# A transformer block on one core: the last channel half of the result in pieces of 384 and 128 columns in place of 256 and 256, the stores of both shared out over two queues

## The chip, the cores and the metric

The kernel runs on one core of one Trainium2 chip. The metric is the device time of one execution in microseconds (us). The kernel before took 307.04 us as the median of three timed runs (306.98, 307.04 and 307.05).

## What is computed

A small causal convolution with a per-channel filter is added to x, and a conditioned transformer block (modulated layer norm, attention with 16 heads, modulated layer norm, feed-forward net with GELU) is added to that. Cut to what the change touches, the end of it:

```python
x = x + gate1 * attn_out
x2 = _ln(x) * (1.0 + scale2) + shift2
h = jax.nn.gelu(x2 @ ffn_w1 + ffn_b1, approximate=False)
x = x + gate2 * (h @ ffn_w2 + ffn_b2)
return x
# and around it, with x of 32 batches x 32 tokens x 256 channels:
x = x + _L0_cond_ref(x, cond_2048[:, None, :])
x = x + _L1_cond_ref(x, cond_2048, ...)
```

## The kernel before

Everything is kept with channels on the partitions: the 256 channels are two channel halves of 128 (index `ct`), the 1024 tokens are two token halves of 512 (index `n`). The engines' streams are written out by hand and tied together by semaphores, so the order of the code is the order of each engine.

A product with more than 11 bits of mantissa is built from three TensorE products of rounded values (type `F32R`): low weights times high activations, high weights times low activations, high times high. In the second product of the feed-forward net (`ffn2`, lines 1241 to 1243) these three run for each of the eight hidden tiles k, so that one piece of the result costs 24 matmuls, each with a weight load of its own of 128 x 128 elements, all adding into one bank.

The result is made in five pieces, listed in `FFN2_PIECES` (line 206): token half 0 in two pieces of 512 columns (one for each channel half), token half 1 with channel half 0 in one of 512, and token half 1 with channel half 1 in two pieces of 256 columns, the first into bank `YB[1]`, the second into `PB[0]`. TensorE runs pieces 2, 3 and 4 one after another at the very end, with no wait between them. The two last are called the front piece (3) and the back piece (4) here.

When a piece's last matmul is done, VectorE works on it with three instructions: `gated` adds the bias and multiplies by the gate (line 889), then adds the residual (line 895), and `turn` transposes blocks of 32 x 32 into `turned` (line 900) and raises `s_turn`. VectorE takes the pieces in order, 2, 3, 4, and has nothing else at the end.

`store_blocks` (line 213) writes one of the four 32-channel strips of a piece to HBM; a piece thus needs four DMAs, each of 32 partitions, cut into runs of 128 bytes. The stores of pieces 0 to 2 are issued by SP (SyncE) as soon as `s_turn` allows. Of the front piece all four are issued by ACT (ScalarE), which has no other work left; of the back piece two are issued by SP and two by ACT, behind ACT's four of the front piece. The last instruction of SP waits until all 20 stores have landed.

Of the kernel before, what the change touches and what calls it, by code (L numbers as in the profile page):

```python
# [11 lines left out]
P = 128  # L12
# [4 lines left out]
def cond_resid_block_kernel(nc, x, cond, ada_w, ada_b, qkv_w, qkv_b, out_w, out_b,  # L17
# [5 lines left out]
    B, T, C = x.shape  # L23
# [7 lines left out]
    HT = TOK // HALVES  # L31
# [39 lines left out]
    with ExitStack() as ctx:  # L71
# [3 lines left out]
        def sem(name):  # L75
            return ctx.enter_context(nc.semaphore(name))
# [57 lines left out]
        PB, S_BANK, OB, YB = banks[0:3], banks[3], banks[4:6], banks[6:8]  # L134
# [33 lines left out]
        s_turn = sem("result_blocks_turned")  # L168
# [22 lines left out]
        def ln_sq(n, ct):  # L191
            if n < NC:
# [9 lines left out]
        ADA_BANKS = [PB[0][:, P:2 * P], S_BANK[:, 2 * P:3 * P], S_BANK[:, 3 * P:4 * P]]  # L202
        ADA_STEPS = [1, 3, 4]

        ALL, FRONT, BACK = slice(0, HT), slice(0, HT // 2), slice(HT // 2, HT)
        FFN2_PIECES = [(0, 0, YB[0][:, ALL], ALL), (0, 1, YB[1][:, ALL], ALL), (1, 0, YB[0][:, ALL], ALL),
                       (1, 1, YB[1][:, FRONT], FRONT), (1, 1, PB[0][:, FRONT], BACK)]

        x_v = x.rearrange("(n q) t c -> (q t) n c", q=QB)
        out_v = out.rearrange("(n q) t c -> (q t) n c", q=QB)  # L210
# [2 lines left out]
        def store_blocks(eng, n, ct, i, toks):  # L213

            b0, b1 = (n * HT + toks.start) // T, (n * HT + toks.stop) // T
            c0 = ct * P + T * i
            eng.dma_start(out[b0:b1, :, c0:c0 + T].rearrange("b t c -> t b c"),
                          turned[T * i:T * (i + 1), CT * n + ct, toks].rearrange("t (b c) -> t b c", c=T))\
                .then_inc(s_out, 16)
# [3 lines left out]
        @block.sync  # L223
        def _(sp):
            def load_x(n):
                t0, nt = CHUNKS[n][0] // P, CHUNKS[n][1] // P
                sp.dma_start(xtok[:, t0:t0 + nt, :], x_v[:, t0:t0 + nt, :]).then_inc(s_x[n], 16)

            def load_adaw(i, c0, c1):
                sp.dma_start(adaw[:, :, c0:c1], ada_w.rearrange("(k p) n -> p k n", p=P)[:, :, c0:c1])\  # L230
                    .then_inc(s_adaw[i], 16)

            def load_qkv(U, i):
                if U:
                    sp.wait_ge(s_wlo[i], 2 * U)
                c0 = (U % NG) * PIECE + i * INNER
                sp.dma_start(raw[:, 1024 * i:1024 * (i + 1)].rearrange("p (k n) -> p k n", k=CT),
                             qkv_v[:, :, c0:c0 + PIECE]).then_inc(s_raw[i], 16)

            def load_out(U):  # L240
                if U:
                    sp.wait_ge(s_wlo[3], 2 * U)
                r0 = (U % NG) * PIECE
                sp.dma_start(raw[:, 3072:4096].rearrange("p (h n) -> p h n", h=GH),
                             out_w[r0:r0 + PIECE, :].rearrange("(h p) n -> p h n", p=P)).then_inc(s_raw[3], 16)

            load_x(0)
            load_x(1)
            load_adaw(0, 0, ADA1 * P)
            load_x(2)  # L250
            for at, src in ((B_QKV, qkv_b), (B_ADA, ada_b), (B_OUT, out_b), (B_F1, ffn_b1), (B_F2, ffn_b2)):
                n = src.shape[0] // P
                sp.dma_start(rows[at:at + n, :], src.rearrange("(n p) -> n p", p=P)).then_inc(s_row[1], 16)
            for i in range(3):
                load_qkv(0, i)
            load_out(0)
            load_adaw(1, ADA1 * P, ADA * P)
            for U in range(1, NU):
                for i in range(3):
                    load_qkv(U, i)  # L260
                load_out(U)

            w1_v = ffn_w1.rearrange("(k p) n -> p k n", p=P)
            w2_v = ffn_w2.rearrange("(k p) n -> p k n", p=P)
            for i in range(3):
                if i == 2:
                    sp.wait_ge(s_xs, CT)
                    for c in range(CT):
                        sp.dma_start(late_raw[:, c, :].rearrange("p (k n) -> p k n", k=2),
                                     w2_v[:, 4 + 2 * c:6 + 2 * c, :]).then_inc(s_late, 16)  # L270
                sp.wait_ge(s_wlo[i], 2 * NU)
                dst = raw[:, 1024 * i:1024 * (i + 1)]
                if i < 2:
                    sp.dma_start(dst, w1_v[:, i, :]).then_inc(s_raw[i], 16)
                else:
                    sp.dma_start(dst.rearrange("p (k n) -> p k n", k=4), w2_v[:, 0:4, :]).then_inc(s_raw[i], 16)

            for n, ct in ((0, 0), (0, 1), (1, 0)):
                sp.wait_ge(s_turn, CT * n + ct + 1)
                for i in range(P // T):  # L280
                    store_blocks(sp, n, ct, i, ALL)
            sp.wait_ge(s_turn, 5)
            for i in range(2):
                store_blocks(sp, 1, 1, i, BACK)
            sp.wait_ge(s_out, 16 * (5 * P // T))

        @block.gpsimd
# [79 lines left out]
        def _(a):  # L367
# [148 lines left out]
            def hidden(n, m):  # L516
                a.wait_ge(s_f1, MT * n + m + 1)

                if MT * n + m >= 4:
                    a.wait_ge(s_hlo[m % 2], (MT * n + m - 4) // 2 + 1)  # L520
                a.activation(hf[:, m % 4, :], PB[m % 3][:, :], ACT.Gelu,
                             bias=bT[:, B_F1 + m:B_F1 + m + 1]).then_inc(s_hf, 1)
                a.wait_ge(s_hf, MT * n + m + 1)
                a.activation(hh[:, m, :], hf[:, m % 4, :], ACT.Copy).then_inc(s_hhi, 1)
# [16 lines left out]
            x1_high(4)  # L541
            for m in range(MT):
                hidden(1, m)
            a.wait_ge(s_turn, 4)
            for i in range(P // T):
                store_blocks(a, 1, 1, i, FRONT)
            a.wait_ge(s_turn, 5)
            for i in range(2, P // T):
                store_blocks(a, 1, 1, i, BACK)

        @block.vector
        def _(v):
# [750 lines left out]
```

## Time and profile before

| | us |
|---|---|
| median of the timed runs | 307.04 |
| the profiled execution | 307.26 |
| its span, first to last instruction | 305.4 |
| TensorE busy | 298.0 (98%) |
| weight loads busy | 251.5 (82%) |
| VectorE busy | 181.3 (59%) |
| ScalarE busy | 172.5 (56%) |
| GpSimd busy | 121.4 (40%) |

The profile gives busy times of each engine, the chain of work that ended last, and with the trace behind it every instruction's start and duration. The granted clock of TensorE was 1.00 (2.4 GHz) over the stretch in question. The profiled execution took 307.26 us, 1.8 us more than its span of 305.4 us; it is 0.22 us above the median of the timed runs.

### The profile page before, as it was taken

The numbers are of one execution on the slowest core, as the hardware profiler recorded it, in microseconds if no ns is written. First come the engines' busy times: TensorE is split into PE (matmuls) and PEld (weight loads), VectorE is DVE, ScalarE is ACT, GpSimd is POOL, SyncE is SP. The second block draws the span as 40 slices with busy tenths as digits, with TensorE's granted clock in tenths as the row PEclk, the third lists the DMA queues.
The fourth block names the chain that finished last, engine by engine and source line by source line (L and its number), as shares of the span: only waits on it lengthen the run. The fifth ranks groups of instructions, "written<-read, shape, count | busy, mean of one in ns | idle before, by whom it ended". The sixth has DMA issues, their size and how long they took to land.

```text
span 305.4 us, 6186 instructions
## 1 busy us (share of the span) xinstructions
PE 298.0 (98%) x2608; PEld 251.5 (82%) x2608; DVE 181.3 (59%) x315; ACT 172.5 (56%) x313; POOL 121.4 (40%) x104
## 2 busy tenths in 40 slices
PE   7999999999999999999999999999999999999994
PEld 7886987878898888888888888888888888878884
DVE  3996697997866648462446673350721364758433
ACT  5943477534762766475377736743763694624910
POOL 5205839331911552173327134630816381310410
PEclk9999999999999999999999999999999999999999
DMA  7902332500160062007003400430090000000304
GB/s 230 368 31 70 105 104 65 145 0 2 38 239 0 4 196 80 2 2 275 3 2 101 176 0 2 162 115 0 4 338 6 2 0 3 0 1 2 69 0 69
DMA packets 22427, 23.00 MB, mean 75 GB/s; under 512 B 9240, under 2 KB 15488, under 8 KB 22400
## 3 DMA queue, kind: packets, MB, share of 16 engines
q1 hardware_dynamic: 20720, 22.39, 22.6%
q10 hardware_dynamic: 1680, 0.23, 0.4%
q8 instruction: 20, 0.33, 0.4%
q14 instruction: 7, 0.06, 0.1%
HBM read 21.57 MB, written 1.05 MB: 74 GB/s over the span
## 4 chain that ended last, share of the span: by engine, by line
PE 90%; DVE 8%; issue 1%; ACT 0%; POOL 0%; DVEq 0%; POOLq 0%
PE bank L1030 17%; PE bank L1031 16%; PE bank L1032 16%; PE bank L1117 9%; DVE xc L585 5%; PE bank L1038 5%; PE bank L1040 5%; PE bank L1039 5%; PE bank L1101 3%; PE bank L1241 3%; PE bank L1243 2%; PE bank L1242 2%; PE bank L969 1%; PE bank L1009 1%; PE bank L989 1%
## 5 line engine op out<-in xcount | busy, mean ns | idle before, releaser
L306 POOL TENSOR_TENSOR wl<-raw,wh 128x512 fp32r<-128x512 f32 x70 | 96.0, 1397 | 119.3 <-ACT wh L379 101.4
L430 ACT ACTIVATE pool<-bank,bT 128x512 f32<-128x512 f32 x56 | 38.5, 688 | 52.3 <-PE bank L1032 52.3
L1030 PE MATMUL bank<-x1h,wl 128*128 128x512 f32 (+1 forms) x174 | 65.7, 378 | 0.1
L1031 PE MATMUL bank<-x1l,wh 128*128 128x512 f32 (+1 forms) x174 | 64.6, 371 | 0.0
L1032 PE MATMUL bank<-x1h,wh 128*128 128x512 f32 (+1 forms) x174 | 64.5, 371 | 0.0
L725 DVE SCALAR_TENSOR_TENSOR ol<-bank,bT,oh 128x512 fp32r<-128x512 f32 x32 | 23.9, 749 | 31.9 <-ACT oh L455 31.1
L585 DVE SCALAR_TENSOR_TENSOR xc<-x,condT,xc 128x496 f32<-128x496 f32 (+27 forms) x80 | 42.1, 597 | 0.1
L379 ACT ACTIVATE wh<-raw 128x512 fp32r<-128x512 f32 x70 | 39.8, 622 | 0.0
L1030 PEld LDWEIGHTS bank<-x1h,wl 128*128 128x128 f32 x174 | 32.8, 188 | 6.6 <-issue 0.7
L1032 PEld LDWEIGHTS bank<-x1h,wh 128*128 128x128 f32 x174 | 32.8, 188 | 5.7
L1031 PEld LDWEIGHTS bank<-x1l,wh 128*128 128x128 f32 x174 | 32.8, 189 | 5.3
L1117 PEld LDWEIGHTS bank<-pt,pool 128*128 128x128 f32 x256 | 32.1, 191 | 2.0 <-issue 0.3
L1117 PE MATMUL bank<-pt,pool 128*128 128x128 f32 x256 | 32.5, 275 | 0.0
L455 ACT ACTIVATE oh<-bank,bT 128x512 fp32r<-128x512 f32 x32 | 22.0, 686 | 10.1 <-PE bank L1117 10.1
L1030 PE MATMUL bank<-oh,wl 128*128 128x512 f32 x64 | 26.6, 415 | 0.2 <-DVE ol L725 0.2
L1038 PE MATMUL bank<-wh,x1l 128*128 128x512 f32 x64 | 25.9, 405 | 0.0
L1040 PE MATMUL bank<-wh,x1h 128*128 128x512 f32 x64 | 25.0, 391 | 0.0
L1032 PE MATMUL bank<-oh,wh 128*128 128x512 f32 x64 | 25.0, 391 | 0.0
L1031 PE MATMUL bank<-ol,wh 128*128 128x512 f32 x64 | 25.0, 390 | 0.0
L1039 PE MATMUL bank<-wl,x1h 128*128 128x512 f32 x64 | 25.0, 390 | 0.0
L697 DVE TENSOR_REDUCE mx<-bank 128x16 f32<-128x512 f32 x8 | 5.5, 692 | 32.4 <-PE bank L1101 32.4
L720 DVE STREAM_TRANSPOSE pt<-pnorm 32x512 f32<-32x512 f32 (+1 forms) x36 | 23.2, 643 | 1.2
(137 smaller groups left out, 427.7 us busy)
## 6 DMA issues: line engine op xcount, KB each, us to landing
raw<-in_L_cond_qkv_w_dram SPq DMA_DIRECT2D x24, 512.0 KB, 5.3
raw<-in_L_cond_out_w_dram SPq DMA_DIRECT2D x8, 512.0 KB, 3.6
raw<-in_L_cond_ffn_w_dram SPq DMA_DIRECT2D x3, 512.0 KB, 6.2
adaw<-in_L_cond_ada_w_dram SPq DMA_DIRECT2D x1, 1024.0 KB, 10.4
out_dram<-pool SPq DMA_DIRECT2D x12, 64.0 KB, 1.9
xtok<-in_x_dram SPq DMA_DIRECT2D x2, 256.0 KB, 3.1
adaw<-in_L_cond_ada_w_dram SPq DMA_DIRECT2D x1, 512.0 KB, 5.4
xtok<-in_x_dram SPq DMA_DIRECT2D x1, 512.0 KB, 6.2
```

Of the source, the lines that this page charges most:

```text
L306: g.tensor_tensor(wl[:, cols], raw[:, cols], wh[:, cols].bitcast(F32), ALU.subtract)\
L379: a.activation(wh[:, cols], raw[:, cols], ACT.Copy).then_inc(s_whi[i], 1)
L430: a.activation((q_sb if j < GH else k_sb)[:, j % GH, :], src, ACT.Identity, bias=bias(U, j // GH, j % GH)).then_inc(s_ev, 1)
L585: m = v.scalar_tensor_tensor(out=acc[:, :, j:], in0=xs[:, :, :T - j], scalar=w, in1=(acc if i else xs)[:, :, j:], op0=ALU.mult, op1=ALU.add)
L725: v.scalar_tensor_tensor(out=ol[:, h, :], in0=OB[h % 2][:, :], scalar=bT[:, row:row + 1], in1=oh[:, h, :].bitcast(F32), op0=ALU.add, op1=A ...
L1030: pe.matmul(dst, wl[:, w_cols], a_hi, start=start, stop=False)
L1031: pe.matmul(dst, wh[:, w_cols], a_lo, start=False, stop=False)
L1032: return pe.matmul(dst, wh[:, w_cols], a_hi, start=False, stop=stop)
L1038: pe.matmul(dst, x1l[:, kt, tk], wh[:, wc], start=(kt == 0), stop=False)
L1039: pe.matmul(dst, x1h[:, kt, tk], wl[:, wc], start=False, stop=False)
L1040: m = pe.matmul(dst, x1h[:, kt, tk], wh[:, wc], start=False, stop=(kt == CT - 1))
L1117: m = pe.matmul(OB[h % 2][:, t * P:(t + 1) * P], v_sb[:, t, h * P:(h + 1) * P], pt[:, h, t, :], start=True, stop=True)
```

## The change

Three things move. The front piece grows from 256 to 384 columns and the back piece shrinks from 256 to 128, in `FRONT`, `BACK` and the bank's slice. The four stores of the front piece are now shared, two by SP and two by ACT, in place of four by ACT. The stores of the back piece are shared as before, two and two. Nothing before the front piece's first matmul is touched.

```diff
-        ALL, FRONT, BACK = slice(0, HT), slice(0, HT // 2), slice(HT // 2, HT)
+        ALL, FRONT, BACK = slice(0, HT), slice(0, HT - P), slice(HT - P, HT)
         FFN2_PIECES = [(0, 0, YB[0][:, ALL], ALL), (0, 1, YB[1][:, ALL], ALL), (1, 0, YB[0][:, ALL], ALL),
-                       (1, 1, YB[1][:, FRONT], FRONT), (1, 1, PB[0][:, FRONT], BACK)]
+                       (1, 1, YB[1][:, FRONT], FRONT), (1, 1, PB[0][:, 0:P], BACK)]
@@ SP
-            sp.wait_ge(s_turn, 5)
-            for i in range(2):
-                store_blocks(sp, 1, 1, i, BACK)
+            for step, toks in ((4, FRONT), (5, BACK)):
+                sp.wait_ge(s_turn, step)
+                for i in range(2):
+                    store_blocks(sp, 1, 1, i, toks)
             sp.wait_ge(s_out, 16 * (5 * P // T))
@@ ACT
-            a.wait_ge(s_turn, 4)
-            for i in range(P // T):
-                store_blocks(a, 1, 1, i, FRONT)
-            a.wait_ge(s_turn, 5)
-            for i in range(2, P // T):
-                store_blocks(a, 1, 1, i, BACK)
+            for step, toks in ((4, FRONT), (5, BACK)):
+                a.wait_ge(s_turn, step)
+                for i in range(2, P // T):
+                    store_blocks(a, 1, 1, i, toks)
```

On TensorE, at the end of the program, the last rows of the kernel before are matmuls of the back piece (moving tile `hh` or `hl`, weights from `wl`, `wh` and, for the upper four hidden tiles, `late_lo` and `late_hi`):

```order
1102 L1241 MATMUL bank<-hh,wl 128x256
1103 L1242 MATMUL bank<-hl,wh 128x256
1104 L1243 MATMUL bank<-hh,wh 128x256
1105 L1241 MATMUL bank<-hh,late_lo 128x256
1106 L1242 MATMUL bank<-hl,late_hi 128x256
```

The same rows of the kernel after:

```order
1102 L1240 MATMUL bank<-hh,wl 128x128
1103 L1241 MATMUL bank<-hl,wh 128x128
1104 L1242 MATMUL bank<-hh,wh 128x128
1105 L1240 MATMUL bank<-hh,late_lo 128x128
1106 L1241 MATMUL bank<-hl,late_hi 128x128
```

The number of matmuls and their order stay as they were (1118 rows either way); only their width changes, to 128 columns here and to 384 in the 24 matmuls ahead of them.

On ACT, at the end of the program, before and after (`pool` is the memory that `turned` lies in, and the last two numbers of a store's shape are batches x 32 channels):

```order
177 L524 ACTIVATE hh<-pool 128x512
178 L217 DMA out_dram<-pool 32x8x32 x6
179 L71 UNCONDITIONAL_BRANCH
```

```order
177 L525 ACTIVATE hh<-pool 128x512
178 L217 DMA out_dram<-pool 32x12x32 x2
179 L217 DMA out_dram<-pool 32x4x32 x2
180 L71 UNCONDITIONAL_BRANCH
```

On SP, the difference at the end of its program:

```order
 L217 DMA out_dram<-pool 32x16x32 x12
-L217 DMA out_dram<-pool 32x8x32 x2
+L217 DMA out_dram<-pool 32x12x32 x2
+L217 DMA out_dram<-pool 32x4x32 x2
```

SP gets two stores of the front piece ahead of its two of the back piece, and ACT has two fewer.

## Rows read from the trace of the kernel before

**Rows 1.** The page: busy time by engine, and the chain that ended last.

```profile
PE 298.0 (98%) x2608; PEld 251.5 (82%) x2608; DVE 181.3 (59%) x315; ACT 172.5 (56%) x313; POOL 121.4 (40%) x104
...
PE 90%; DVE 8%; issue 1%; ACT 0%; POOL 0%; DVEq 0%; POOLq 0%
```

**Rows 2.** Chain of waits from 301 us on: start us, us, what.

```profile
301.11 0.13 PE bank L1243
301.25 0.02 issue
301.27 0.49 DVE x L889
301.76 0.02 issue
301.79 0.43 DVE x L895
302.22 0.02 issue
302.25 0.45 DVE pool L900
```

**Rows 3.** Timeline of TensorE, pieces 2 to 4: start us, us, engine, line, instruction, tiles.

```profile
289.78 0.40 PE L1241 MATMUL bank<-hh,wl 128*128 128x512 f32 x1
...
295.14 0.39 PE L1243 MATMUL bank<-hh,late_hi 128*128 128x512 f32 x1
...
295.37 0.28 PE L1241 MATMUL bank<-hh,wl 128*128 128x256 f32 x1
...
298.22 0.28 PE L1241 MATMUL bank<-hh,wl 128*128 128x256 f32 x1
...
300.95 0.28 PE L1243 MATMUL bank<-hh,late_hi 128*128 128x256 f32 x1
```

**Rows 4.** Timeline, weight loads in bursts of 8 records, 128 x 128 elements.

```profile
24.87 0.97 PEld L984 LDWEIGHTS bank<-ones,x 128*128 128x128 f32 x8 [0.93 <-ACT x L410]
...
10.81 0.93 PEld L1142 LDWEIGHTS bank<-ident,xtok 128*128 128x128 f32 x8
...
60.69 0.97 PEld L1117 LDWEIGHTS bank<-pt,pool 128*128 128x128 f32 x8
...
57.14 1.98 PEld L1117 LDWEIGHTS bank<-pt,pool 128*128 128x128 f32 x16
```

**Rows 5.** TensorE by line: weight loads and matmuls, duration ns min/median/max, forms.

```profile
L1241 PEld LDWEIGHTS bank<-hh,wl x20: 187/188/189, 265.8 to 299.2; 128*128 128x128 f32 x20
...
L984 PEld LDWEIGHTS bank<-ones,x x8: 186/192/192, 24.9 to 25.6; 128*128 128x128 f32 x8
L984 PE MATMUL bank<-ones,x x8: 250/250/271, 24.9 to 25.7; 128*128 128x1 f32 x8
...
L1101 PEld LDWEIGHTS bank<-pool x1024: 106/109/113, 47.8 to 240.6; 128*32 128x32 f32 x171
```

**Rows 6.** Timeline of VectorE on pieces 2 and 3.

```profile
295.57 0.75 DVE L889 SCALAR_TENSOR_TENSOR x<-bank,bT,adaT 128x512 f32<-128x512 f32 x1 [3.52 <-PE bank L1243]
296.36 0.69 DVE L895 TENSOR_TENSOR x<-x,xc 128x512 f32<-128x512 f32 x1
297.08 0.71 DVE L900 STREAM_TRANSPOSE pool<-x 128x512 f32<-128x512 f32 x1
...
298.42 0.48 DVE L889 SCALAR_TENSOR_TENSOR x<-bank,bT,adaT 128x256 f32<-128x256 f32 x1 [0.63 <-PE bank L1243]
```

**Rows 7.** VectorE grouped by line and shape: xcount, busy us, mean ns, idle before.

```profile
L632 DVE STREAM_TRANSPOSE vt<-bank 128x128 f32<-128x128 f32 x3 | 0.9, 315 | 0.4 <-PE bank L989 0.4
L684 DVE TENSOR_TENSOR adaT<-bank,bT 128x128 f32<-128x128 f32 x3 | 0.8, 278 | 0.0
```

**Rows 8.** Timeline of the stores' issue, by queue.

```profile
297.82 1.94 SPq L217 DMA_DIRECT2D out_dram<-pool  x4
...
299.88 1.87 ACTq L217 DMA_DIRECT2D out_dram<-pool  x4
...
302.72 0.81 SPq L217 DMA_DIRECT2D out_dram<-pool  x2
302.72 0.88 ACTq L217 DMA_DIRECT2D out_dram<-pool  x2
```

**Rows 9.** Trace by line, second store of each queue; DMA issues, median us to landing.

```profile
L217 SPq DMA_DIRECT2D out_dram<-pool x1: 452/452/452, 303.1 to 303.1; - x1
L217 ACTq DMA_DIRECT2D out_dram<-pool x1: 476/476/476, 303.1 to 303.1; - x1
...
DMA to landing us min/median/max: 1.7/1.8/1.9
...
out_dram<-pool SPq DMA_DIRECT2D x4, 64.0 KB, 1.9
...
out_dram<-pool ACTq DMA_DIRECT2D x4, 32.0 KB, 1.7
```

**Rows 10.** What SP's queue waited for from 301 us: us in total, times, longest.

```profile
SPq L217 <- DVE pool L900: 2.9, 1, 2.9
SPq L71 <- DMA out_dram<-pool: 1.5, 1, 1.5
```

**Rows 11.** Busy time by stretch; the last two numbers are DMA share, GB/s.

```profile
302.80:303.20 0.40, 0.00 (x0) 0.00 (x0) 0.00 (x0) 0.00 (x0) 0.00 (x0) 1.00 0.00 0
303.20:303.60 0.40, 0.00 (x0) 0.00 (x0) 0.00 (x0) 0.00 (x0) 0.00 (x0) 1.00 0.07 12
303.60:304.00 0.40, 0.00 (x0) 0.00 (x0) 0.00 (x0) 0.00 (x0) 0.00 (x0) 1.00 0.90 146
304.00:304.40 0.40, 0.00 (x0) 0.00 (x0) 0.00 (x0) 0.00 (x0) 0.00 (x0) 1.00 0.86 138
304.40:304.80 0.40, 0.00 (x0) 0.00 (x0) 0.00 (x0) 0.00 (x0) 0.00 (x0) 1.00 0.22 32
```

## The prediction

> **What bounds the kernel now.** I read the busy times first: TensorE is busy for 98% of the span, and 90% of the chain that ended last is TensorE's [rows 1]. So time is made or lost at two kinds of places: where TensorE itself gets longer, and behind its last matmul, where nothing covers the work. The change touches just these two. The chain of waits from 301 us on shows what stands behind the last matmul: it starts at 300.95 us [rows 3], VectorE takes the bank over at 301.27 us, and its three instructions of 0.49, 0.43 and 0.45 us end at 302.70 us [rows 2]. The stores of the back piece are issued from 302.72 us on, two on each queue [rows 8]. The second one of each queue starts at 303.1 us and the slower of these takes 1.9 us to land, at 305.0 us [rows 9]; SP's last wait, 1.5 us for a store [rows 10], ends there, and the span at 305.4 us. So the tail is 0.3 us of hand-over, 1.4 us of VectorE and 2.7 us of store.
>
> **TensorE.** The sum of the columns stays as it was: 24 x (256 + 256) becomes 24 x (384 + 128). The question is what a matmul of each width costs, from start to start.
> - 512 columns: piece 2 runs from 289.78 to 295.37 us, 24 matmuls, 0.233 us each [rows 3].
> - 256 columns: the front piece runs from 295.37 to 298.22 us, 0.119 us each [rows 3].
> - 384 columns: no row; halfway between the two, 0.176 us. The front piece takes 24 x 0.176 = 4.22 us in place of 2.85, and the back piece begins at 295.37 + 4.22 = 299.59 us.
> - 128 columns of this type: no row either. The same line carried on gives 0.233 - 3 x 0.038 = 0.062 us per matmul. But every matmul here loads 128 x 128 weights of its own, and the trace shows how fast such loads follow each other when the matmuls between them are short. At line 984 the matmuls have **one** column, and yet the eight loads start (0.97 - 0.19) / 7 = 0.111 us apart [rows 4, 5]. The loads of the transposes at line 1142, whose matmuls are 128 columns wide, start (0.93 - 0.14) / 7 = 0.113 us apart, taking their own duration as the load record's 0.14 us; those of line 1117 0.111 us, or (1.98 - 0.19) / 15 = 0.119 us in a double burst [rows 4]. A load of the back piece's kind has the same duration, 188 ns, as those of line 984, 192 ns [rows 5], so the type of the weights shows no difference. A load of 32 columns has 109 ns [rows 5]: the 96 columns more cost 0.08 us, so the load goes by its columns and not by the matmul's.
>
> So at 256 columns the matmul (0.119 us) still just covers the load (0.111 us), and at 128 columns the load is what is left. I take 0.113 us, of line 1142, since it is the row with one record for each instruction and 128 moving columns; 0.111 and 0.119 us stay as bounds. The last matmul then starts 23 x 0.113 = 2.60 us behind 299.59, at 302.19 us.
>
> The Trainium skill, page "TensorE: Matmul & The Clock Gate", section "LDWEIGHTS (loading the stationary operand)", says a load costs its column count over 1.2 GHz, 107 ns for 128 columns, and its section "Weight-path perf modes" says that the fast weight load is not given to FP32; by that, the trace agrees within 4 to 6 ns. The same page's section "Back-to-back issue gap" gives 81 ns for a matmul of 128 columns in a stream with its loads; with that the last matmul would start 0.7 us earlier and nearly the whole loss would be gone. The page's other examples there are bf16, and no row here goes below 0.11 us with a load of 128 columns.
>
> **Hand-over.** From the start of a piece's last matmul to VectorE's start it is 0.43 us at 512 columns (295.14 to 295.57) and 0.32 us at 256 (300.95 to 301.27) [rows 2, 3, 6]; carried on, 0.27 us at 128. VectorE starts on the back piece at 302.46 us in place of 301.27: **+1.19 us**.
>
> **VectorE.** The front piece is now 384 wide. It begins 0.37 us behind the front piece's last matmul (299.42), at 299.79 us, and its three instructions, halfway between 0.75 and 0.48, 0.69 and 0.43, 0.71 and 0.45 us [rows 2, 6], end with their gaps at 301.62 us: 0.8 us before the back piece is there, so this costs nothing; the cover is the slow back piece itself. For the back piece each instruction is shorter by the same step: 0.48 to 0.35, 0.43 to 0.29, 0.45 to 0.32 us. The 128-column rows of VectorE, 0.278 us for an addition and 0.315 us for a block transpose [rows 7], agree. That is **-0.40 us**; the last transpose ends at 303.49 us.
>
> **Stores.** Moved from ACT to SP are two stores of the front piece. SP has issued its four of piece 2 by 299.8 us (297.82 + 1.94) [rows 8] and then waits, so they go out at 301.6 us, on both queues at once, and the second of each is issued by 302.5 us. ACT's four took 1.87 us from 299.88 us on, ended at 301.75 us, and stood in nobody's way, since the back piece came at 302.70 us [rows 8]: sharing them gains nothing by itself. It is needed by the new pieces, since four in a row from 301.6 us would have ended at 303.5 us, just when the back piece is ready. The data of the front stores, landing about 1.9 us after the second issue at 302.0 us, is gone by 303.9 us; the first data of a store moves some 0.6 us after its issue (issue at 302.72 us, share 0.07 in 303.20 to 303.60) [rows 8, 11], so that of the back piece at about 304.1 us. No collision, with 0.2 us to spare.
>
> The back piece's stores are 16 KB each in place of 32 KB. The second on each queue still starts 0.38 us after the first. Landing took 1.9 us for 64 KB, 1.7 us for 32 KB alone on a queue and 1.9 us for the slower one with two queues busy [rows 9]. The DMA engines' busy stretch of these four stores, about 0.9 of 1.2 us [rows 11], is halved at best, but the issues 0.38 us apart don't shrink. I take 1.7 us for the last landing, **-0.2 us**; bounds are 0 and -0.4.
>
> **Sum.** +1.19 - 0.40 - 0.20 = +0.59 us. The profiled execution of 307.26 us with its span of 305.4 us would be 307.85 with 306.0; against the median of 307.04 us, 0.22 us lower than the profiled one, that is **307.6 us**. A difference of 0.2% (0.61 us) is about what a measurement of this kernel can tell from no change, so this forecast stands just at that line. Its own range: loads at 0.111 to 0.119 us give -0.05 to +0.14, the landing -0.2 to +0.2, the width of 384 and the VectorE steps +-0.1: +0.3 to +1.0, 307.3 to 308.1 us.
>
> **Rivals.**
> - *The weight loads hide after all.* If loads of this type follow each other faster than those of lines 984 and 1142, the back piece goes by its columns, 0.062 us per matmul. Its last matmul starts at 299.59 + 1.43 = 301.02 us, and now VectorE is the bound, since the front piece holds it until 301.62 us. Its end is then 301.64 + 0.35 + 0.29 + 0.32 + 0.05 = 302.65 us, 0.05 us earlier than now, and with the smaller stores -0.25 us: 306.8 us. If the front piece's stores, which then are only 1 us ahead, crowd the back ones, it is no gain. For it speaks that no row shows this type with fewer than 256 columns, against it that the load records have the same length. It decides once a load takes less than about 0.09 us. By the 81 ns of the Trainium skill's page on TensorE, cited above, the case would end at about 306.9 us. This is the case that ends as not slower; more than 0.2% faster it could only be if the stores' landing shrank by over 0.5 us.
> - *A short matmul of this type runs at the pace of full float32.* Line 1117 is full float32 with 128 columns; each of its instructions leaves two records, so 0.22 us per instruction [rows 4]. If TensorE gives its one-record pace only to wide tiles, the back piece takes 23 x 0.22 = 5.1 us to its last start, VectorE starts at 305.1 us, +3.8, and the end is +3.2 us: 310.2 us. Everything of this type in the trace is 256 or 512 wide, so that nothing speaks directly against it; what makes it less likely is that two records come from two passes over the weights, which a width does not call for. The Trainium skill, page "FP8 and Floating Point Precision", section "TensorE Precision Notes", ties the four passes to true FP32 and not to a width. No run here shows it yet.
> - *Loads and short matmuls don't overlap fully.* Between these, if each matmul adds some of its own time to the load, say 0.15 us as a pair, the end is 23 x 0.037 = 0.85 us later than forecast: 308.5 us.
>
> **Chances.** Forecast (load pace) 0.62, rival of hidden loads 0.10, float32 pace 0.17, partial overlap 0.08, anything else 0.03. The range of 306.7 to 308.5 us takes in all but the float32 pace and the rest. By 0.2% (below 306.43, above 307.65): the forecast's case is split nearly evenly, 0.30 within and 0.32 above; hidden loads 0.08 within and 0.02 below; the others above but for 0.02. Together faster 0.03, within 0.40, slower 0.57.
>
> **What would show it.** In the profile after: starts of the last 24 matmuls 0.11 to 0.12 us apart (0.06, 0.15 or 0.22 for the rivals), starts of the 24 before them 0.176 us apart; VectorE's first instruction of the back piece at about 302.5 us with some 0.8 us of idle time before it; its last transpose ending at about 303.5 us; front stores on both queues at 301.6 us; SP's last wait ending at about 305.6 us. The prediction is wrong if the 24 short matmuls take other than 2.6 to 2.9 us, or if the last wait for a store ends more than 2.4 or less than 1.9 us after the last transpose (2.3 us now).

## The result: 0.16% slower, and the profile after

The changed kernel takes 307.47 us as the median of 22 runs (307.41 to 307.55), the kernel before 306.99 us (306.90 to 307.06, 22 runs on the same chips). The ratio is 1.0016 with a 95% interval of 1.0010 to 1.0022: 0.48 us slower, a small loss. It is inside the 0.2% that the prediction took as the line between "no change" and "slower", though the interval reaches just over that line. The forecast was 307.6 us.

The page after answers to [rows 1]. TensorE and its weight loads are busy for 0.8 and 1.2 us longer, nothing else has moved:

```profile
PE 298.8 (98%) x2608; PEld 252.7 (83%) x2608; DVE 181.3 (59%) x315; ACT 172.6 (56%) x313; POOL 121.4 (40%) x104
...
PE 90%; DVE 7%; issue 1%; ACT 0%; POOL 0%; DVEq 0%; POOLq 0%
```

The timeline of TensorE after answers to [rows 3] (start us, us, engine, line, instruction; every line number is one lower than before):

```profile
295.05 0.34 PE L1240 MATMUL bank<-hh,wl 128*128 128x384 f32 x1
295.23 0.34 PE L1241 MATMUL bank<-hl,wh 128*128 128x384 f32 x1
...
299.10 0.34 PE L1242 MATMUL bank<-hh,late_hi 128*128 128x384 f32 x1
299.28 0.22 PE L1240 MATMUL bank<-hh,wl 128*128 128x128 f32 x1
299.33 0.28 PE L1241 MATMUL bank<-hl,wh 128*128 128x128 f32 x1
299.45 0.27 PE L1242 MATMUL bank<-hh,wh 128*128 128x128 f32 x1
...
301.79 0.27 PE L1242 MATMUL bank<-hh,late_hi 128*128 128x128 f32 x1
```

The front piece's first matmul stands at 295.05 us here and at 295.37 us in the profile before. Nothing ahead of it was changed, and two profiled executions of one kernel differ by nearly as much: when the changed kernel was profiled once more (e9 below), that matmul stood at 295.31 us. So the stretch is best counted from that first matmul. The front piece takes (299.28 - 295.05) / 24 = 0.176 us per matmul. Of the back piece the first matmul still profits from a load that ran beside a wide one (its record is 0.22 us long in place of 0.27 or 0.28) and is followed after 0.05 us; then they come (301.79 - 299.33) / 22 = 0.112 us apart. Their loads do the same, each 0.19 us long:

```profile
301.51 0.19 PEld L1240 LDWEIGHTS bank<-hh,late_lo 128*128 128x128 f32 x1
301.62 0.19 PEld L1241 LDWEIGHTS bank<-hl,late_hi 128*128 128x128 f32 x1
301.73 0.19 PEld L1242 LDWEIGHTS bank<-hh,late_hi 128*128 128x128 f32 x1
```

VectorE's timeline after answers to [rows 2, 6], and the stores with what SP's queue waited for answer to [rows 8 to 10]:

```profile
299.48 0.62 DVE L888 SCALAR_TENSOR_TENSOR x<-bank,bT,adaT 128x384 f32<-128x384 f32 x1 [2.01 <-PE bank L1242]
300.13 0.56 DVE L894 TENSOR_TENSOR x<-x,xc 128x384 f32<-128x384 f32 x1
300.72 0.58 DVE L899 STREAM_TRANSPOSE pool<-x 128x384 f32<-128x384 f32 x1
302.10 0.35 DVE L888 SCALAR_TENSOR_TENSOR x<-bank,bT,adaT 128x128 f32<-128x128 f32 x1 [0.81 <-PE bank L1242]
302.49 0.29 DVE L894 TENSOR_TENSOR x<-x,xc 128x128 f32<-128x128 f32 x1
302.81 0.31 DVE L899 STREAM_TRANSPOSE pool<-x 128x128 f32<-128x128 f32 x1
```

```profile
297.50 6.45 SPq L217 DMA_DIRECT2D out_dram<-pool  x8
...
SPq L71 <- DMA out_dram<-pool: 1.3, 1, 1.3
...
out_dram<-pool SPq DMA_DIRECT2D x2, 48.0 KB, 1.9
out_dram<-pool ACTq DMA_DIRECT2D x2, 48.0 KB, 2.1
out_dram<-pool SPq DMA_DIRECT2D x2, 16.0 KB, 1.5
out_dram<-pool ACTq DMA_DIRECT2D x2, 16.0 KB, 1.6
```

VectorE is idle for 0.81 us ahead of the back piece. SP's last store is issued by 297.50 + 6.45 = 303.95 us, and the wait of 1.3 us behind it ends with the last landing. The views round such waits to 0.1 us; in the trace itself, which keeps whole nanoseconds, the last store lands at 305.04 us before and at 305.21 us after. With the trace's own times, counted from the front piece's first matmul:

| us from there to | before | after | difference |
|---|---|---|---|
| start of the last matmul | 5.58 | 6.74 | +1.16 |
| VectorE starts on the back piece | 5.90 | 7.05 | +1.15 |
| last transpose done | 7.32 | 8.08 | +0.76 |
| last store landed | 9.67 | 10.16 | +0.49 |

So TensorE lost 1.16 us, VectorE gave back 0.40 and the stores 0.27. The sum of +0.49 us is what the medians say (+0.48). Two further profiles repeat the last line within 0.01 us: 9.66 us for e1, whose pieces are those of before, and 10.17 us for e9, the changed kernel again.

### The profile page after: what moved, and what is told of

Read it like the earlier page. It is cut to its first block, busy times and chain, and to the rows that moved or that the text cites. A ratio compares the mean times of both kernels' runs of the same rounds, so it can differ in the third digit from the quotient of the medians.

```text
span 305.6 us, 6186 instructions
## 1 busy us (share of the span) xinstructions
PE 298.8 (98%) x2608; PEld 252.7 (83%) x2608; DVE 181.3 (59%) x315; ACT 172.6 (56%) x313; POOL 121.4 (40%) x104
## 4 chain that ended last, share of the span: by engine, by line
PE 90%; DVE 7%; issue 1%; ACT 0%; POOL 0%; DVEq 0%; POOLq 0%
PE bank L1029 17%; PE bank L1030 16%; PE bank L1031 16%; PE bank L1116 9%; DVE xc L584 5%; PE bank L1037 5%; PE bank L1038 5%; PE bank L1039 5%; PE bank L1100 3%; PE bank L1240 3%; PE bank L1242 3%; PE bank L1241 3%; PE bank L968 1%; PE bank L1008 1%; PE bank L988 1%
```

## Experiments

Each was timed beside the kernel before on the same chip (e1 to e7 on one, e8 and e9 on another), where the kernel before had a median of 307.23 or 307.24 us. The difference is given against that. In e9 below the changed kernel was timed once more in this way: +0.50 us. The 95% interval of such a ratio reaches about 0.3 us to either side, so differences of 0.1 or 0.2 us are not clear of noise by the medians alone; for these the trace, counted from the front piece's first matmul, is the better witness, and a table at the end of this section has both.

**What sets the pace of the narrow matmuls (e5).** The back piece with half of every weight load, so that half of its output channels are left out:

```diff
+                if piece == 4:
+                    bank, w_hi, w_lo = bank[0:P // 2], w_hi[:, 0:P // 2], w_lo[:, 0:P // 2]
                 pe.matmul(bank, w_lo, hh[:, k, toks], start=(k == 0), stop=False)
```

> The changed kernel, but in the back piece only the first 64 of the 128 weight columns are loaded and used (the other 64 output channels of that piece are left out). If the load sets the pace, the 24 matmuls of 128 columns come 0.06 to 0.07 us apart in place of 0.111, VectorE becomes the bound (back piece right behind the front piece's transpose), 0.7 to 0.8 us faster than the changed kernel, 0.2 to 0.3 us faster than before. If short matmuls of this type have a floor of their own, they stay 0.111 us apart and the time stays as in the changed kernel.

The timeline of TensorE and, below it, of the weight loads in e5:

```profile
299.56 0.22 PE L1242 MATMUL bank<-hh,wl 128*64 128x128 f32 x1
299.62 0.22 PE L1243 MATMUL bank<-hl,wh 128*64 128x128 f32 x1
299.68 0.22 PE L1244 MATMUL bank<-hh,wh 128*64 128x128 f32 x1
...
300.94 0.22 PE L1244 MATMUL bank<-hh,late_hi 128*64 128x128 f32 x1
```

```profile
299.62 0.14 PEld L1244 LDWEIGHTS bank<-hh,wh 128*64 128x64 f32 x1
299.69 0.13 PEld L1242 LDWEIGHTS bank<-hh,wl 128*64 128x64 f32 x1
```

The moving tile is as wide as in the changed kernel, only the load is halved, and the matmuls come (300.94 - 299.56) / 23 = 0.060 us apart in place of 0.112. So it is not the 128 moving columns that take 0.112 us; the load sets the pace, and without it they cost what the straight line through 256 and 512 columns says (0.062 us). Halving the load also halves the outputs of each matmul; that this isn't the reason is shown by e6 below, where a narrow matmul with a full load takes 0.06 us once its load is hidden. With TensorE out of the way VectorE is the bound: it goes from the front piece to the back one without a pause. Measured 307.08 us, 0.15 us under before and 0.65 us under the changed kernel's +0.50, a little less than was expected. The trace has the rest: the last store lands 2.35 us behind the last transpose, as before the change, and not 2.08 us as in the changed kernel. SP and ACT had issued the front piece's stores only just ahead, and the first store of the back piece took 0.46 and 0.52 us to issue in place of 0.32 and 0.37.

**Other widths (e3, e4).** `BACK` of 192 and of 64 columns:

```diff
-        ALL, FRONT, BACK = slice(0, HT), slice(0, HT - P), slice(HT - P, HT)
+        ALL, FRONT, BACK = slice(0, HT), slice(0, HT - 192), slice(HT - 192, HT)
```

> The changed kernel with pieces of 320 and 192 columns. If weight loads set the pace of narrow matmuls, 192 columns cost 0.111 us each like 128: TensorE 24 x (0.148 + 0.111) = 6.2 us, +0.5 on before; VectorE -0.2, hand-over and stores -0.15: +0.1 to +0.2 us on before. If the pace goes by columns with a surcharge only for 128 (0.09 us at 192), TensorE stays at 5.7 us and the end is 0.3 to 0.4 us earlier than before.

> The changed kernel with pieces of 448 and 64 columns. Load theory: 64 columns still cost 0.111 us each, TensorE 24 x (0.204 + 0.111) = 7.6 us, +1.9 on before; VectorE's three instructions 0.6 us shorter than before, hand-over and stores 0.4 us: +0.8 to +1.0 us on before. If the pace goes by columns, TensorE stays at 5.7 us, VectorE's front piece (2.1 us) becomes the bound, and the time is within 0.5 us of before.

The last matmuls of e3, and then of e4:

```profile
301.21 0.27 PE L1240 MATMUL bank<-hh,late_lo 128*128 128x192 f32 x1
301.32 0.28 PE L1241 MATMUL bank<-hl,late_hi 128*128 128x192 f32 x1
301.44 0.27 PE L1242 MATMUL bank<-hh,late_hi 128*128 128x192 f32 x1
```

```profile
302.48 0.28 PE L1240 MATMUL bank<-hh,late_lo 128*128 128x64 f32 x1
302.59 0.28 PE L1241 MATMUL bank<-hl,late_hi 128*128 128x64 f32 x1
302.70 0.28 PE L1242 MATMUL bank<-hh,late_hi 128*128 128x64 f32 x1
```

192, 128 and 64 columns all come 0.11 us apart. A floor that only 128 columns had would not show at 192, where the columns alone would take some 0.09 us. Measured +0.10 us for 320 and 192 (307.33) and +0.92 us for 448 and 64 (308.16), both as the load theory had it (+0.1 to +0.2 and +0.8 to +1.0). The narrower the last piece, the more each of its 24 matmuls pays for columns that it doesn't have, and VectorE and the stores give back less than that at each step.

**Each half of the change alone (e1, e2).** e1 has the shared stores with pieces of 256 and 256, e2 the widths of 384 and 128 with all four front stores on ACT, that is the hunks of the diff above one by one.

> Pieces of 256 and 256 as before, only the stores of the front piece shared over both queues. My theory (the prediction's): sharing gains nothing by itself, since ACT's four stores of the front piece had ended 1 us before the back piece was ready: within 0.1 us of the kernel before, last wait for a store 1.5 us, back piece's second store landing 1.9 us after its issue. Rival (ACT's queue was still in the way of the back piece): 0.1 to 0.3 us faster than before, with a shorter landing.

> Pieces of 384 and 128, the four front stores all on ACT as before. Theory: TensorE and VectorE as in the changed kernel (back piece's 24 matmuls 0.111 us apart, VectorE's last transpose at the same place), but ACT issues front stores for 1.9 us from the end of the front piece's transpose, so it is free only about 0.1 us after the back piece is ready, and front data is still moving: 0.1 to 0.3 us slower than the changed kernel, +0.6 to +0.8 us on the kernel before. Rival (the queue doesn't matter): equal to the changed kernel, +0.5.

e1: 307.25 against 307.23 us, no difference, and SP's last wait is still 1.5 us. e2: 307.87 us, +0.64. In e2 ACT's queue issues without a pause from the front piece's transpose to the end:

```profile
301.40 2.90 ACTq L217 DMA_DIRECT2D out_dram<-pool  x6
```

Its last store ends at 304.3 us, 0.3 us behind SP's (304.03 us), where in the changed kernel the two queues end 0.07 us apart. Counted from the front piece's first matmul, e2's last store lands at 10.30 us in place of 10.16, and the medians, +0.64 on one chip and +0.50 on another, differ by the same 0.14 us. So the whole loss comes from the widths, and the sharing is worth about 0.14 us, but only with these widths; by the medians alone that would not be clear of noise.

**Hiding the loads behind wide matmuls (e6, e7).** The first six matmuls of the back piece alternate with the last six of the front piece (e6), or the first nine with pieces of 320 and 192 (e7):

```diff
-            for piece in (2, 3, 4):
-                for k in range(MT):
-                    ffn2(piece, k)
+            for k in range(MT):
+                ffn2(2, k)
+            for k in range(MT - 2):
+                ffn2(3, k)
+            for k in range(2):
+                for _ in zip(ffn2_steps(4, k), ffn2_steps(3, MT - 2 + k), strict=True):
+                    pass
+            for k in range(2, MT):
+                ffn2(4, k)
```

> The changed kernel, but the first 6 of the back piece's 24 matmuls (hidden tiles 0 and 1) alternate with the last 6 of the front piece's. Load theory: next to a matmul of 384 columns two loads (0.22 us) hide behind two matmuls (0.24 us), so each pair takes 0.24 us in place of 0.29: 0.3 us faster than the changed kernel, +0.2 us on before; VectorE just keeps up (18 matmuls of 0.111 us behind the front piece against 1.8 us of its work). Rival (a short matmul costs 0.111 us wherever it stands): equal to the changed kernel.

> Pieces of 320 and 192 columns, stores shared, and the first 9 of the back piece's matmuls alternating with the last 9 of the front piece's. Load theory: a pair takes 0.24 us in place of 0.26, 0.2 us less than pieces of 320 and 192 in a row: -0.1 to 0 us on the kernel before. Rival: as pieces of 320 and 192 in a row.

This expectation failed: 307.77 us (+0.53) and 307.31 us (+0.07), each what the same widths cost in a row. The timeline of e6, matmuls first, then the loads:

```profile
298.51 0.22 PE L1240 MATMUL bank<-hh,wl 128*128 128x128 f32 x1
298.57 0.39 PE L1240 MATMUL bank<-hh,late_lo 128*128 128x384 f32 x1
298.80 0.22 PE L1240 MATMUL bank<-hl,wh 128*128 128x128 f32 x1
298.86 0.39 PE L1240 MATMUL bank<-hl,late_hi 128*128 128x384 f32 x1
299.09 0.22 PE L1240 MATMUL bank<-hh,wh 128*128 128x128 f32 x1
```

```profile
298.33 0.19 PEld L1240 LDWEIGHTS bank<-hh,wl 128*128 128x128 f32 x1
298.51 0.19 PEld L1240 LDWEIGHTS bank<-hh,late_lo 128*128 128x128 f32 x1
298.62 0.19 PEld L1240 LDWEIGHTS bank<-hl,wh 128*128 128x128 f32 x1
298.80 0.19 PEld L1240 LDWEIGHTS bank<-hl,late_hi 128*128 128x128 f32 x1
```

The narrow matmul now takes 0.06 us, since its load ran beside the wide one before it. But the wide matmul behind it is 0.05 us slower (0.39 in place of 0.34 us long, 0.23 us to the next start in place of 0.176): its own load could start only with the narrow matmul, at 298.51 us, not earlier beside the wide one. A pair still takes 0.29 us = 0.111 + 0.176, and in e7 a pair of 192 and 320 columns takes 0.26 us (298.05 - 297.79) = 0.111 + 0.148. VectorE was not what held e6 up: it had finished the front piece and stood idle for 0.14 us before the back piece came. So in these streams loads run one matmul ahead and no more; a stream costs, matmul by matmul, the larger of its columns and the next load, and with loads all of one size the order doesn't matter.

**Less work behind the last matmul (e8).** The pieces are 256 and 256 again, the stores shared as in e1. What lies behind TensorE's end is VectorE's three instructions, so one is taken away: the residual over the gate, plus the bias, goes into the back piece's bank by two matmuls with the identity as weights (a high and a low part), prepared while VectorE and ScalarE are idle. Then gating is one multiplication:

```diff
+                    pe.matmul(FFN2_PIECES[4][2], ident_r[:, :], uh[:, :], start=True, stop=False)
+                    pe.matmul(FFN2_PIECES[4][2], ident_r[:, :], ul[:, :], start=False, stop=False)
...
-            gated(4)
+            v.wait_ge(s_f2, 5)
+            v.tensor_tensor(by_batch(part(x0, 1, back)), by_batch(FFN2_PIECES[4][2]), ada(GATE2, 1, back), ALU.mult)
```

> Pieces of 256 and 256, stores shared, and for the back piece the residual and the bias are added on TensorE: (residual / gate + bias), split into a high and a low part while VectorE and ScalarE have nothing else, goes through two more matmuls of 256 columns with the identity as weights, and VectorE's addition of the residual behind the last matmul falls away. Theory: behind TensorE's end only instructions on the path count, and a matmul of 256 columns hides its load: +2 x 0.119 = +0.24 us on TensorE, -0.45 us on VectorE, 0.2 us faster than the kernel before, 0.7 us faster than the changed one. Rival: the preparation (three VectorE instructions, two on ScalarE) comes late and holds up the pieces' gating or the first of the two matmuls, and the gain is lost.

> The changed kernel once more, beside the kernel before and the folded one on the same chip: +0.4 to +0.6 us on the kernel before.

VectorE's timeline in e8, first the preparation, then the tail:

```profile
291.98 0.19 DVE L921 RECIPROCAL rg<-adaT 128x8 f32<-128x8 f32 x1
292.21 0.42 DVE L924 TENSOR_TENSOR u<-xc,rg 128x256 f32<-128x256 f32 x1
293.21 0.49 DVE L927 SCALAR_TENSOR_TENSOR ul<-u,bT,uh 128x256 fp32r<-128x256 f32 x1 [0.58 <-ACT uh L553]
...
301.54 0.42 DVE L934 TENSOR_TENSOR x<-bank,adaT 128x256 f32<-128x256 f32 x1 [1.66 <-PE bank L1263]
302.00 0.45 DVE L908 STREAM_TRANSPOSE pool<-x 128x256 f32<-128x256 f32 x1
```

VectorE's part of the tail is 0.90 us in place of 1.42, the two matmuls at 298.25 and 298.37 us cost 0.24 us, and the preparation is over at 293.7 us, long before piece 2 is there. e8 took 307.04 us (307.03 to 307.11, 11 runs), the kernel before beside it 307.23 us (307.18 to 307.30, 21 runs), the changed kernel 307.73 us (e9). Against the changed kernel it is 0.69 us faster, and the two intervals don't overlap. Against the kernel before the medians are 0.19 us apart and the ranges of the runs don't overlap, but the ratio's interval, 0.9985 to 1.0003, still holds 1. So a gain is likely and not shown beyond doubt; the trace has the last store 0.24 us earlier. e8 divides by the gate, so it is only for inputs whose gate isn't zero.

All runs against the kernel before. The trace's column is the time from the front piece's first matmul to the landing of the last store, 9.67 us before:

| | medians, us | trace, us |
|---|---|---|
| e1, stores only | +0.02 | -0.01 |
| e2, widths only | +0.64 | +0.63 |
| e3, 320 and 192 | +0.10 | +0.10 |
| e4, 448 and 64 | +0.92 | +0.93 |
| e5, half loads | -0.15 | -0.17 |
| e6, alternating | +0.53 | +0.53 |
| e7, alternating, 320 and 192 | +0.07 | +0.10 |
| e8, folded | -0.19 | -0.24 |
| e9, the changed kernel again | +0.50 | +0.50 |

## Why the prediction was right, step by step

- *Pace of the narrow matmuls.* Taken from the loads of line 1142 (0.113 us), with 0.111 us of line 984 as the lower bound; measured 0.112 us. The choice of rows was right, and e5 and e6 showed that the reason was too. A line through the widths, 0.062 us, would have put the last start 1.1 us too early. The Trainium skill, page "TensorE: Matmul & The Clock Gate", section "Back-to-back issue gap", names no operand type beside the 81 ns that the prediction quotes from it; no stream here shows 81 ns with a full load.
- *Width 384.* 0.176 us forecast, 0.176 measured.
- *First narrow matmul and hand-over.* The prediction counted a full load for all 23 steps, but the load of the first narrow matmul was hidden, so the last start came 2.51 and not 2.60 us behind the first. The hand-over was forecast at 0.27 us and measured at 0.31 us (301.79 to 302.10), because the last matmul's record holds its wait for its load: it is 0.27 us long, where the first narrow one, whose load was hidden, has 0.22 us. These two slips go opposite ways and half cancel, which is luck. VectorE's start: +1.19 forecast, +1.15 measured.
- *VectorE.* -0.40 forecast, -0.40 measured. It stood idle 0.81 us ahead of the back piece, as forecast (0.8).
- *Stores.* -0.20 forecast, -0.27 measured: from the last transpose to the last landing it is 2.08 us in place of 2.35. The last landing took 1.6 us where 1.7 was taken. The front stores landed after 2.1 us on ACT's queue, longer than the 1.9 taken, but their data had stopped moving at about 303.4 us, and the back piece's began at about 303.9 us: no collision, as forecast.
- *Sharing the stores gains nothing by itself.* e1 showed just that, and e2 that it saves about 0.14 us with the narrow back piece, where the prediction named ACT's queue as the cost without it.
- *Rivals.* Hidden loads would have shown 0.06 us between matmuls, the float32 pace 0.22, a partial overlap 0.15. None is there. The sum of the float32 rival has a slip: 23 x 0.22 us and a hand-over of 0.27 us put VectorE's start at 304.9 and not 305.1 us, so its end would be some 0.15 us below the stated 310.2 us. Nothing hung on it.

The terms give +0.49 us in the trace and the medians +0.48 to +0.50 us, against +0.59 forecast: 0.04 us less of TensorE and hand-over, 0.07 us more from the stores. The forecast stood 0.02 us from the line of 0.2%, and "slower" was given the larger chance (0.57 against 0.40 for "within"); the result fell 0.13 us under that line, so the less likely side came, by an error of size and not of mechanism. The signs of being wrong were not met, one of them narrowly: the 24 short matmuls took 2.62 us, with the last one's 0.11 us counted in, against a lower bound of 2.6 us.

## What to carry to other kernels

To shorten the tail behind TensorE's end by a narrower last piece can pay only as long as the piece's matmuls take longer than their weight loads; look in the trace for a row with short matmuls and full loads, and take its pace as the floor, here 0.111 us for 128 x 128, which 256 columns (0.119 us) just cover. Below that every matmul paid the load in full, and putting wide matmuls between didn't help. What shortened the tail here, by 0.2 us at most, was one instruction less behind the last matmul, its work taken over by two matmuls wide enough to cover their loads (e8). Sharing stores over two queues was worth something only where one queue was still issuing when the last piece was ready (e2), and nothing where it wasn't (e1).

## What the runs showed that was not expected

In these streams a weight load runs beside the matmul just ahead and never further ahead: with 128 and 384 columns in turn each pair took 0.29 us, the sum of a load (0.111 us) and a wide matmul (0.176 us), although both loads (0.22 us) would have fitted beside both matmuls (0.24 us). The Trainium skill, page "TensorE: Matmul & The Clock Gate", section "Step-by-step: what each phase is for", describes a 64-deep window that pulls loads ahead of matmuls in flight, where the row groups don't conflict or the load goes to a background weight buffer. It doesn't say how many loads can be ahead; the traces here, with full 128 x 128 weights, show one.

The pace of the load goes by its columns: 0.060 us or less at 64 columns (e5, where the 128 moving columns may be what is left), 0.111 us at 128. The load records, 0.11 us at 32 columns and 0.19 us at 128, have 0.14 us at 64, on the line between.

The hand-over from the last matmul's start to VectorE was 0.43 us at 512 columns, 0.32 at 256 and 0.31 or 0.32 at 192, 128 and 64: below 256 columns it no longer falls. The reason lies in the matmul's record. Where VectorE is waiting, it starts about 0.04 us behind the end of the last matmul's record at each of these widths, and below 256 columns the record itself, 0.27 or 0.28 us, no longer shrinks, since it holds the wait for the load; with the load hidden the first matmul of a piece has 0.25, 0.22 and 0.19 us at 192, 128 and 64 columns. The ends of matmul records are modelled, so this is a reading of the records and no separate test. So a narrow last matmul with a full load doesn't hand over sooner either.
